# Attention on pairs of heads with split operands, and a router on rows that are not yet normalised

## The reference

```python
# layer 0, mixture: the router
x = _layernorm(x)                                   # eps 1e-5
probs = softmax(x @ w_router)                       # 8 experts
top_vals, top_idx = top_k(probs, 2)
out += w_e * ((silu(x @ w_gate[e] * 0.5) * (x @ w_up[e])) @ w_down[e] * 0.25)

# layer 1: NH=32 query heads, KVH=4, HD=128, S=256, B=4
q, k, v = rope(h @ Wq), rope(h @ Wk), h @ Wv
scores = einsum('bqhd,bkhd->bhqk', q, k) / sqrt(128)
attn = softmax(where(causal, scores, -1e9))
o = einsum('bhqk,bkhd->bqhd', attn, v).reshape(B, S, NH * HD) @ Wo
x = resid + o
```

## Time and profile before

| | |
|---|---|
| median of 3 runs | 1094.86 us (1094.78 to 1096.74) |
| the profiled execution, its own time | 1095.35 us |
| its span | 1093.5 us |
| mean granted clock of TensorE | 0.945 |
| busy: TensorE, VectorE, ScalarE, GpSimd | 1001.4, 870.9, 640.0, 431.6 us |
| share of TensorE in the chain that ended last | 72% |

### The profile page before, as it was taken

The page is one execution under the profiler, slowest core; times in us unless marked ns, Lnnn a source line. Parts: engine busy times, 40 slices in busy tenths (PEclk is TensorE's granted clock), DMA queues, the critical chain, the costliest instruction groups (busy, mean ns, idle before and its releaser), DMA issues.

```text
span 1093.5 us, 21079 instructions
## 1 busy us (share of the span) xinstructions
PE 1001.4 (92%) x6394; PEld 863.9 (79%) x6394; DVE 870.9 (80%) x2644; ACT 640.0 (59%) x1767; POOL 431.6 (39%) x372
## 2 busy tenths in 40 slices
PE   4798777999994689999999999999989999999997
PEld 2455545799993478999999999999878888888886
DVE  6999997677765889777786777777878878788887
ACT  4789984655552387877777777777843222222221
POOL 5789893543321243323232333212422332232231
PEclk9869887699997599999999999999999999999999
DMA  9700003011115011010101100000000111111111
GB/s 291 256 1 2 1 2 108 29 55 49 47 37 172 2 39 50 1 40 2 49 2 39 35 2 2 1 2 1 26 20 30 44 43 58 43 43 49 52 43 38
DMA packets 49462, 49.30 MB, mean 45 GB/s; under 512 B 4896, under 2 KB 42464, under 8 KB 49376
## 3 DMA queue, kind: packets, MB, share of 16 engines
q1 hardware_dynamic: 45888, 40.83, 11.9%
q0 software_dynamic: 2208, 6.03, 1.9%
q10 hardware_dynamic: 1280, 1.38, 0.4%
HBM read 43.11 MB, written 5.11 MB: 44 GB/s over the span
## 4 chain that ended last, share of the span: by engine, by line
PE 72%; DVE 11%; POOL 7%; ACT 5%; issue 4%; DMA 1%; SPq 0%; DVEq 0%; ACTq 0%; POOLq 0%
PE bank L57 13%; PE bank L58 13%; PE bank L59 13%; PE bank L954 7%; PE bank L975 5%; PE bank L857 4%; PE bank L866 4%; PE bank L878 4%; PE bank L964 3%; POOL rest L1418 3%; PE bank L976 2%; POOL alpha L1421 2%; DVE alpha L1626 1%; PE bank L646 1%; PE bank L933 1%
## 5 line engine op out<-in xcount | busy, mean ns | idle before, releaser
L1483 POOL TENSOR_TENSOR rot_s<-swap,rq 128x512 f32<-128x512 f32 x64 | 88.6, 1385 | 194.7 <-ACT swap L1261 194.6
L1134 ACT ACTIVATE silu<-bank 128x512 f32<-128x512 f32 x66 | 39.4, 598 | 173.6 <-PE bank L59 173.6
L2073 DVE TENSOR_TENSOR o_ring<-bank,o_ring 128x256 fp32r<-128x256 f32 x128 | 54.2, 424 | 80.3 <-ACT o_ring L1290 78.9
L1274 ACT ACTIVATE prob<-prob,pmin 128x128 f32<-128x128 f32 (+1 forms) x256 | 113.3, 447 | 5.5 <-DVE pmin L2054 5.5
L954 PE MATMUL bank<-kv,norm 128*128 128x128 f32 (+1 forms) x512 | 105.8, 330 | 5.2 <-DVE norm L2047 5.2
L1896 DVE SCALAR_TENSOR_TENSOR xs<-bank,wt,xs 128x256 f32<-128x256 f32 x264 | 109.0, 476 | 0.1
L1439 POOL TENSOR_TENSOR gate_r<-gate_w,gate_r 128x256 fp32r<-128x256 f32 x31 | 36.4, 1174 | 177.3 <-ACT gate_r L1127 177.3
L1290 ACT ACTIVATE o_ring<-bank 128x256 fp32r<-128x256 f32 x128 | 48.3, 377 | 76.4 <-PE bank L976 76.3
L57 PE MATMUL bank<-wo_r,o_ring 128*128 128x256 f32 x256 | 82.4, 322 | 0.0
L1874 DVE TENSOR_TENSOR hidf<-silu,bank 128x512 f32<-128x512 f32 x66 | 45.4, 687 | 44.9 <-ACT silu L1134 43.3
L2066 DVE TENSOR_SCALAR prob<-prob,pinv 128x128 f32<-128x128 f32 (+1 forms) x256 | 77.0, 343 | 4.6
(11 more groups left out here) (309 smaller groups left out, 3151.4 us busy)
## 6 DMA issues: line engine op xcount, KB each, us to landing
gate_w<-in_Wg SPq DMA_DIRECT2D x33, 128.0 KB, 2.2
up_w<-in_Wu SPq DMA_DIRECT2D x33, 128.0 KB, 2.3
down_w<-in_Wd SPq DMA_DIRECT2D x33, 128.0 KB, 2.3
w_all<-in_w_gate SPq DMA_DIRECT2D x8, 512.0 KB, 10.6
w_all<-in_w_up SPq DMA_DIRECT2D x8, 512.0 KB, 10.4
w_all<-in_w_down SPq DMA_DIRECT2D x8, 512.0 KB, 10.6
wq_g<-in_Wq SPq DMA_DIRECT2D x4, 1024.0 KB, 5.6
wo_g<-in_Wo SPq DMA_DIRECT2D x4, 1024.0 KB, 5.6
```

Of the source, the lines that this page charges most:

```text
L1274: ins = act.activation(prob[:, u % 4, nt * P:nt * P + (nt + 1) * P], prob[:, u % 4, nt * P:nt * P + (nt + 1) * P], ACT.Exp, bias=pmin[:, u ...
L1483: pool.tensor_tensor(rot_s[:, m % 2].rearrange("p (b n) -> p b n", b=2), swap[:, m % 2].rearrange("p (b n) -> p b n", b=2), bcast(tab[:, 1 ...
```

## The change

In attention: units come in pairs of two heads on the same sequence (`unit_of`). `weigh` takes a pair at once, once in two iterations and now first in an even one; values and probabilities are split into high and low fp32r parts (`vt`, `vt_low`, `probT`, `probT_low`), and a pair takes three matmuls of 512 and three of 256 columns. The low part of the probabilities is a new step of VectorE, `low_T`; `turn` and `weigh` wait for it. `high_out` and `low_out` take a pair at once. ScalarE scales the first 128 columns of the probabilities (`scale_first`), VectorE the other 256.

In the router: `turn_graph` transposes `xs`, not `norm`. The mean is taken out of the weights instead (`router_means`, one subtraction), and the inverse deviation is multiplied onto the logits. The first six tiles (`LEAD`) are routed while the last graph is being transposed. `normalise_graph(3)` comes after the choice, the loads of the first attention weights come before `store_graph(3)`, and the distances `TURN_AT` and `ROUTE_AT` are shorter.

```diff
-        NORM_AT, TURN_AT, ROUTE_AT = (ALL, ALL + 2, ALL + 10), (ALL + 2, ALL + 4, ALL + 11), (ALL + 4, ALL + 6, ALL + 12)
+        NORM_AT, TURN_AT, ROUTE_AT = (ALL, ALL + 2, ALL + 10), (ALL, ALL + 1, ALL + 7), (ALL + 2, ALL + 3, ALL + 8)
...
+        def v_low(t):
+            return vt_low[:, t % 4, t // 4 * 4:t // 4 * 4 + 4, :].rearrange("p t e -> p (t e)")
+        def out_pair(p, part):
+            return o_ring[:, 2 * p % O_RING:2 * p % O_RING + 2, part, :]
...
             blk, rem = divmod(u, BU)
-            return (blk, blk // 2, blk % 2) + divmod(rem, 2)
+            return blk, blk // 2, blk % 2, rem // 4 * 2 + rem % 2, rem // 2 % 2
```

SyncE:

```diff
             sp.dma_start(before[:], before_in).then_inc(S["before_in"], 16)
+            load_queries(0)
+            load_values(0)
             store_graph(B - 1)
             sp.dma_start(rq[:], rope_q).then_inc(S["att_in"], 16)
             sp.dma_start(rk[:], rope_k).then_inc(S["att_in"], 16)
-            load_queries(0)
-            load_values(0)
```

TensorE, router:

```diff
-                    pe.wait_ge(S["norm_done"], NT * b + NT)
+                    pe.wait_ge(S["x1_added"], b + 1)
...
-                                              norm[:, NT * b + nt, c * P:c * P + P], ident[:])
+                                              xs[:, NT * b + nt, c * P:c * P + P], ident[:])
...
+                def router_means():
+                    pe.wait_ge(S["const_in"], 16 * 5)
+                    pe.wait_ge(S["mean_set"], 1)
+                    pe.wait_ge(S["z_copied"], ALL)
+                    for c in range(HC):
+                        mm = pe.matmul(bank[2][:, T * E0:(T + 1) * E0], work[:, 0:P], wr0[:, c, :], start=c == 0, stop=c == HC - 1)
+                    mm.then_inc(S["wr_mean"], 1)
```

TensorE, attention:

```diff
                 def turn(u):
                     pe.wait_ge(S["p_norm"], u + 1)
+                    pe.wait_ge(S["p_scaled"], u + 1)
                     if u >= 1:
-                        pe.wait_ge(S["pT_copied"], u)
+                        pe.wait_ge(S["pT_low"], u)
...
-                def weigh(u):
+                def weigh(p):
+                    blk, g, half, r, b2 = unit_of(2 * p)
                     t = NT * (2 * half + b2)
+                    pe.wait_ge(S["pT_low"], 2 * p + 2)
+                    if p % (BU // 2) == 0:
+                        pe.wait_ge(S["q_taken"], blk * JOBS + 1)
+                    if p >= 1:
+                        pe.wait_ge(S["o_copied"], p)
-                    pe.matmul(O_BANK[:, 0:N], vt[:, t, :], probT[:, u % 2, 0:N], start=True, stop=False)
-                    pe.matmul(O_BANK[:, P:N], vt[:, t + 1, :], probT[:, u % 2, N:N + P],
-                              start=False, stop=True).then_inc(S["o_ready"], 1)
+                    dst = O_BANK.rearrange("p (u n) -> p u n", u=2)
+                    for nt in range(NT):
+                        rows, cols = slice(nt * P, N), slice(nt * N, nt * P + N)
+                        for i, (v, weights) in enumerate(((vt[:, t + nt, :], probT), (vt[:, t + nt, :], probT_low),
+                                                          (v_low(t + nt), probT))):
+                            mm = pe.matmul(dst[:, :, rows], v, weights[:, :, cols],
+                                           start=nt == 0 and i == 0, stop=nt == NT - 1 and i == 2)
+                    mm.then_inc(S["o_ready"], 1)
...
                 for k in range(FIRST, END):
+                    if k % 2 == 0 and 0 <= k - 4 < AU:
+                        weigh((k - 4) // 2)
                     if 0 <= k - 2 < AU:
                         turn(k - 2)
...
-                    if 0 <= k - 3 < AU:
-                        weigh(k - 3)
                     if 0 <= k - 5 < AU:
                         project_out(k - 5)
```

ScalarE:

```diff
+                def scale_first(u):
+                    act.wait_ge(S["p_inv"], u + 1)
+                    act.activation(prob[:, u % 4, 0:P], prob[:, u % 4, 0:P], ACT.Copy, scale=pinv[:, u % 4, 0:1]
+                                   ).then_inc(S["p_scaled"], 1)
...
                 def copy_T(u):
                     act.wait_ge(S["pT_ready"], u + 1)
                     if u >= 2:
-                        act.wait_ge(S["o_ready"], u - 1)
+                        act.wait_ge(S["o_ready"], u // 2)
...
-                def high_out(u):
+                def high_out(p):
+                    act.wait_ge(S["o_ready"], p + 1)
+                    if 2 * p + 2 > O_RING:
+                        act.wait_ge(S["o_used"], 2 * p + 2 - O_RING)
+                    act.activation(out_pair(p, 0), O_BANK.rearrange("p (u n) -> p u n", u=2), ACT.Copy
+                                   ).then_inc(S["o_high"], 1)
...
                 for k in range(FIRST, END):
-                    if 0 <= k - 4 < AU:
-                        high_out(k - 4)
+                    if k % 2 == 0 and 0 <= k - 4 < AU:
+                        high_out((k - 4) // 2)
                     if (q := job_in(k, 1)) is not None:
                         swap_halves(*q)
                     if 0 <= k - 2 < AU:
                         copy_T(k - 2)
+                    if 0 <= k - 1 < AU:
+                        scale_first(k - 1)
                     if 0 <= k < AU:
                         exps(k)
```

VectorE, attention:

```diff
-                        dve.tensor_copy(vt[:, 4 * half:4 * half + 4, :], Q_BANK[n % 2].rearrange("p (t n) -> p t n", t=4)
-                                        ).then_inc(S["q_taken"], 1)
+                        src, high = Q_BANK[n % 2].rearrange("p (t n) -> p t n", t=4), vt[:, 4 * half:4 * half + 4, :]
+                        dve.tensor_copy(high, src).then_inc(S["v_high"], 1)
+                        dve.wait_ge(S["v_high"], blk + 1)
+                        dve.tensor_tensor(vt_low[:, 0:4, 4 * half:4 * half + 4, :].rearrange("p j t e -> p j (t e)"),
+                                          src, high.bitcast(F32), ALU.subtract).then_inc(S["q_taken"], 1)
...
-                    for nt in range(NT):
-                        ins = dve.tensor_scalar(prob[:, u % 4, nt * P:nt * P + (nt + 1) * P],
-                                                prob[:, u % 4, nt * P:nt * P + (nt + 1) * P],
-                                                pinv[:, u % 4, nt:nt + 1], None, ALU.mult)
-                    ins.then_inc(S["p_norm"], 1)
+                    dve.tensor_scalar(prob[:, u % 4, P:3 * P], prob[:, u % 4, P:3 * P],
+                                      pinv[:, u % 4, 1:2], None, ALU.mult).then_inc(S["p_norm"], 1)
+
+                def low_T(u):
+                    dve.wait_ge(S["pT_copied"], u + 1)
+                    dve.tensor_tensor(probT_low[:, u % 2, :], PT_BANK[:, 0:3 * P], probT[:, u % 2, :].bitcast(F32),
+                                      ALU.subtract).then_inc(S["pT_low"], 1)
...
                     if 0 <= k < AU:
                         shift(k)
-                    if 0 <= k - 4 < AU:
-                        low_out(k - 4)
                     if 0 <= k - 1 < AU:
                         normalise(k - 1)
+                    if k % 2 == 0 and 0 <= k - 4 < AU:
+                        low_out((k - 4) // 2)
+                    if 0 <= k - 2 < AU:
+                        low_T(k - 2)
```

VectorE, router:

```diff
+            def scaled_logits(ts, logits, ready, rms, done):
+                R = route[:, 0, ts, 0:E0]
+                dve.wait_ge(ready, 1)
+                dve.wait_ge(S["x_rms"], rms)
+                chain.link(dve.tensor_tensor(R, logits.rearrange("p (t e) -> p t e", e=E0), bcast(rstd[:, ts], 2, E0), ALU.mult))
+                chain.link(dve.tensor_reduce(rcol[:, 0, ts], R, X, ALU.max))
+                dve.tensor_tensor(R, R, bcast(rcol[:, 0, ts], 2, E0), ALU.subtract).then_inc(done, 1)
...
             def router0():
+                scaled_logits(slice(0, LEAD), bank[2][:, 0:LEAD * E0], S["lead_ready"], 2 * B - 1, S["lead_max"])
+                two_largest(slice(0, LEAD), S["lead_exp"])
+                scaled_logits(slice(LEAD, T), bank[3][:, 0:NT * E0], S["logit_ready"], 2 * B, S["rmax_done"])
+                two_largest(slice(LEAD, T), S["rexp_done"])
...
                 dve.scalar_tensor_tensor(weight, chosen, 0.25, padded[:, :, 0:E0], ALU.mult, ALU.mult)
+                normalise_graph(B - 1)
                 dve.wait_ge(S["count_ready"], 1)
```

More of the change, by code:

```diff
@@ L1569, in finish_second, with normalise_graph @@
                 chain.link(dve.tensor_scalar(bT1[:], bT[:], -1.0, None, ALU.add))
+            def normalise_graph(b):
+                dve.wait_ge(S["x_rms"], B + b + 1)
+                for t in (NT * b, NT * b + 1):
+                    dve.tensor_scalar(norm[:, t, :], xs[:, t, :], mv[:, t, 0:1], rstd[:, t:t + 1],
+                                      ALU.subtract, ALU.mult).then_inc(S["norm_done"], 1)
             def graph_attention():
@@ L1703, in graph_attention @@
                         divide(j)
+                    for b in range(B - 1):
+                        if k == NORM_AT[b]:
+                            normalise_graph(b)
```

(18 more changed lines are left out.)

93 lines of the change are left out of this document (37 added, 56 removed).

## The result

The changed kernel takes 1149.4 us (median of 4 runs, 1146.7 to 1151.8) against 1094.8 for the kernel before in the same session: ratio 1.0489, 95% interval 1.0473 to 1.0504. It is slower by 54.6 us; the forecast was 42. The profiled execution took 1150.0 us with a span of 1148.2, 54.7 more than the span before. In the experiments, one execution of act_late (1433.9 us, mean granted clock 0.65) was a slow one and is not in its ratio.

What follows compares the result with a forecast made beforehand. TensorE was taken to bound attention, at 51.91 us a block. 1095.35 plus 45.3 (stalls of 63.2 less 17.9 saved) less 3.3 for the router gave 1137.4, forecast as 1137 us, range 1112 to 1160.

Steps and rivals of the forecast that it cites:

- The chain: Even attention iteration with a swap: `high_out`, swaps, `copy_T`, `low_T` in order let TensorE go on 4.34 us after `weigh` starts.
- the four stalls of 1.58: Even iterations 0, 6, 8, 14 of a block, with swap and no projection, each stall TensorE for 1.58 us.
- the odd ones: Odd iterations 3 and 11, with a swap and no projection, lead to stalls before `weigh` of 1.08 and 0.44 us.
- The saving: TensorE's `weigh` falls from 1.32 to 1.05 us a pair: 0.28 saved over 64 pairs, 17.9 us.
- The first block: First attention block, held by VectorE for a part, where the residuals stand too: some 6 us of stalls.
- it costs nothing: Attention's new unit order moves scores of odd heads one iteration forward; their rotated queries are ready, so no cost.
- The clock: TensorE's clock stays at 1.00 throughout.
- The last block: Last attention block: 6.0 us of stalls from swaps up to iteration 8, and some 3 for its end.
- The router: Measuring, root and normalising leave the chain before the choice: `chosen` comes 3.3 us earlier, bounds 1 and 5.
- (a): Attention: only occupancy counts, the chain is hidden and TensorE stays full: 1074 us, chance 0.10.
- (b): Attention: half the stalls, 31.6 us, giving 1106 us, chance 0.08.
- (c): Attention worse: new matmuls cost 1.32 a pair (1155 us), or stalls lower the clock (1173 us); chance 0.10.

Runs made afterwards that it cites:

- act_late: The changed kernel with ScalarE issuing `high_out` behind `swap_halves` and `copy_T`: 1143.7 us (ratio 1.0432).
- both_late: The changed kernel with ScalarE issuing `high_out` behind `swap_halves` and `copy_T`, and VectorE issuing `low_T` before `low_out`: 1109.5 us (ratio 1.0120).
- one_swap: The changed kernel with the swap as one copy of 128 partitions instead of two of 64, halves not exchanged: 1113.8 us (ratio 1.0181).
- router_only: The kernel before with the change's router and without its attention: 1093.2 us (ratio 0.9976).
- rotate_early: both_late with VectorE's `rotate` before `low_T`: 1112.1 us (ratio 1.0164).
- out_first: rotate_early with TensorE issuing `project_out(k-5)` before `weigh` instead of last in even iterations: 1126.8 us (ratio 1.0276).
- jobs_moved: both_late with the projections at other iterations of the block: 1113.0 us (ratio 1.0142).
- short sines: act_late or both_late with GpSimd multiplying 64 of the 512 sine columns, the rest left zero: 1128.7 us and 1102.9 us respectively.
- swap_mid: both_late with ScalarE's order `copy_T`, swap, `high_out`, `scale_first`, exponentials: 1151.7 us (ratio 1.0512).

## Why the prediction was right

The direction, the mechanism and 42 of the 54.6 us hold. The forecast's sum, cut at the v projections, against the two timelines (us; forecast from its own terms: stalls less 0.28 a pair):

| part | forecast | measured |
|---|---|---|
| gate of the first mixture to v of k = 9 | 4.0 - 0.8 = +3.2 | +5.9 |
| six periods of a block | 48.2 - 13.4 = +34.8 | +42.1 |
| from there to the end | 11.0 - 3.6 = +7.4 | +9.2 |
| start of that gate (router) | -3.3 | -2.5 |
| sum | +42.1 | +54.7 |

- **The chain.** Right, to 0.02 us in every step of an even iteration, and with it the four stalls of 1.58 and the odd ones of 1.08 (measured 1.07) and 0.44 (0.45). That it is the order which makes them is shown by both_late, which changes only orders, and by one_swap, which shortens only what stands in between. The swap started when `high_out` was through and not when its projection was. The Trainium skill, "TensorE: Matmul & The Clock Gate", section "Step-by-step: what each phase is for", keeps ScalarE in order; by that rule the trace agrees.
- **The saving.** Right in kind and too large. `weigh` costs 1.05 to 1.07 a pair as taken. But what it replaced was cheaper: I had read the old `weigh` as the distance to the matmul behind it less 0.12, and that matmul takes longer after an fp32 one (0.21 here, to the 487.48 of the earlier trace rows). TensorE's own work in a block fell by 51.91 - 50.3 = 1.6 and not by 2.24: 0.21 a pair, about 13 in all instead of 17.9. This is some 4.7 of the missing 12.6 us. The prediction held both numbers: by its own steps a pair of iterations goes from 2 x 2.35 to 2.76 + 1.71, which saves 0.23. Its period of 58.1 rests on these, its sum on 0.28 (57.7 a block); with 0.23 the sum would have been 1140. The row of the kernel before behind the old `weigh`, its timeline:

```profile
487.27 0.36 PE L57 MATMUL bank<-wo_r,o_ring 128*128 128x256 f32 x1
```

- **`rotate` behind `low_T`.** The sum has no term for it. The scores of a block's first unit wait for the `rotate` that stands behind the new `low_T`: 0.36 in each of seven blocks, 2.5 in all. Of each 0.36 some 0.19 is the `rotate` being held by GpSimd. The order of units isn't the cause, since the first unit and its query are the same in both orders; the odd heads, of which the prediction said "it costs nothing", don't wait in the steady blocks.
- **The first block.** It was priced at "some 6" without its rows being followed. The miss is in the part up to the v projection of k = 9 (2.7), where TensorE idles for 2.65 before the `weigh` at 392.10 and for 1.12 before the one at 409.35. About 2.5 of it I didn't take apart. The period behind it, with 2.25 before the `weigh` at 425.52, is long in the kernel before too, and adds 0.2.
- **The clock.** Forecast at 1.00 throughout. It is at its lower level for some 3 us three times in attention, from 393.1, 673.0 and 792.4; the last section shows one. The kernel before has none there. The later two cost 1.6 each; the first falls among other waits and has no price of its own.
- **The last block.** Its end was priced some 1 too high: 1.8 is missing there, and the terms above would give 2.9.
- **The router.** From the last residual add to `chosen` it is shorter by 3.8 where 3.3 was forecast, and 2.5 arrive at the mixture; router_only gives 2.6. From the first residual add to the last it takes 39.2 us before, and 41.6 in the changed kernel and in router_only: as far as one trace of each can tell, the shorter distances give a part back there. The end of the first add alone lies between 139.8 and 143.6 in the traces of the changed kernel and its variants, which don't differ up to there, so no single trace gives the router's worth to better than a us or two, and the 0.8 in the table is inside that.
- These terms are 4.7, 2.5, 2.5 and 0.2, 3.2, 0.8, less 1: 12.9 against 12.6 missing, which is within their rounding.
- **The range.** 1112 to 1160 held, in part by luck: 1155 stood for a pair at 1.32, and the pair cost 1.05; other terms, all to the slow side, filled that room. (That bound also left out the 5.6 of `low_T`.)
- **The rivals.** (a) and (b) fall by the period; for (c), the pair's price is 1.05, and the clock gave a small part of what (c) had. 0.954 is the granted clock over the span, against 0.945 before.

What keeps a wait of about 0.6 before `weigh` of iteration 12 in both_late, rotate_early, out_first and jobs_moved can be read from the rows: two chains of nearly the same length end there. One is ScalarE's, whose swap of iteration 11 stands ahead of `copy_T`; the other VectorE's, with the two copies of v, one of them new. jobs_moved took the swap away and left 0.53 to VectorE. No run takes both away. GpSimd's hold isn't in it (0.62 with short sines); it is in the wait before the transposes, 0.42 in both_late and 0.94 in rotate_early. That an order exists which gives 50.3 a block with one bank for the transposes isn't shown.

## What to carry to other kernels

Before work is moved from the engine that bounds the kernel to engines with room, write down the loop through the shared bank, in the order in which each engine's queue has its steps, with the rows' own durations, and compare it with the bounding engine's own iteration; occupancy alone said 1074 here and the loop said 1137. In a software pipeline, a consumer that is issued first in an iteration should read what was finished an iteration ago; `high_out` read what was being made, and everything behind it waited. And when one wait is mended, look for every second condition of the same instruction: in swap_mid a wait of 1.4 came back from another releaser at the same size, and in jobs_moved one of 0.6 came back as 0.5, by another chain to the same releaser.

## What the hardware showed that I had not expected

**VectorE held up by GpSimd.** A scaling of 256 fp32 columns from SBUF to SBUF takes 0.35 us alone and up to 1.46 when an operation of GpSimd is under way; it ends 0.15 after GpSimd's (act_late: 542.26 and 542.11). It isn't slowed in proportion, it waits. The `rotate`s that take 0.87 in the changed kernel, additions with both inputs in SBUF, each end 0.55 after GpSimd's sines. Sums above 0.35: 11.7 us in the changed kernel, 34.2 in act_late, 4.2 with short sines. Operations that read PSUM didn't show it (`low_T` has a mean of 0.55 and a longest of 0.56 in the changed kernel). The Trainium skill, "SBUF — State Buffer", section "SBUF: two separate sides", says that the two engines share a pair of ports as an exclusive lock, held for a whole instruction by whoever starts first, where VectorE's operation is in a mode with two ports or has two inputs in SBUF. By that rule the trace agrees for the `rotate`s, which have two inputs, and for the scalings if they are in such a mode, which no run here shows. The prediction should have had it as a cost of a faster loop.

**The clock after short waits.** Windows of the changed kernel (us; busy of PE, PEld, DVE, ACT, POOL; clock; DMA; GB/s):

```profile
652.00:654.00 2.00, 2.00 (x20) 2.00 (x19) 2.00 (x4) 0.89 (x5) 0.70 (x1) 1.00 0.00 0
672.00:674.00 2.00, 1.82 (x8) 1.40 (x8) 1.96 (x8) 1.01 (x4) 0.00 (x0) 0.74 0.04 8
674.00:676.00 2.00, 2.00 (x6) 1.51 (x6) 1.97 (x9) 1.06 (x5) 0.00 (x0) 0.50 0.00 0
676.00:678.00 2.00, 2.00 (x14) 1.77 (x13) 0.22 (x1) 0.00 (x0) 0.00 (x0) 0.90 0.00 0
```

And TensorE's timeline there:

```profile
671.88 0.52 PE L994 MATMUL bank<-ident,prob 128*128 128x128 f32 x3 [1.42 <-DVE probT_low L2134]
...
673.31 0.99 PE L57 MATMUL bank<-actT_r,wqk_r 128*128 128x512 f32 x1
674.10 0.63 PE L58 MATMUL bank<-actT_r,wqk_r 128*128 128x512 f32 x1
674.53 0.63 PE L59 MATMUL bank<-actT_r,wqk_r 128*128 128x512 f32 x1
```

After a wait of 1.42 us the clock falls to its lower level, 1.2 GHz, for some 3 us: matmuls of 512 columns then start 0.43 apart instead of 0.23. From these transposes to the next ones (678.06) it is 6.18 us, where it is 4.60 a block earlier (613.24 to 617.84): 1.6 lost. Of five steady periods one has this (60.23 against 58.64); the others have the same waits and keep 2.4 GHz. Two more stretches of the changed kernel show it (392 to 398 and 791 to 797 us, at 0.72 each), and the second of these costs 1.6 as well. The kernel before and router_only, whose TensorE hardly waits in attention, have 1.00 from 390 to 1090 us; two single waits of 1.8 in the kernel before (393.66 and 819.88) brought no fall. That the waits bring the clock down is read from this and not tested by itself; if so, stalls of this kind cost more than their length now and then, and not each time.
